# Cross-attention with a quantised feed-forward: the front of each batch one step earlier, and programs of their own for the last three steps

## The chip, the cores and the metric

One core of one Trainium2 chip runs the whole kernel in one launch. The metric is the device time of that launch in microseconds. The engines are PE (TensorE, matmuls and turns by matmul), DVE (VectorE), ACT (ScalarE), POOL (GpSimd) and SP (SyncE, which here only issues DMAs). Each has its own program and runs it in order; they meet by semaphores.

## The reference

Eight batches of 256 tokens by 512 features go through an attention layer and a feed-forward layer, each with a residual:

```python
x = x + attention(layernorm(x), ctx)      # 32 heads of 16, 8 groups: 4 query heads share one K, V head
x = x + ffn(layernorm(x))

# attention: q = X @ Wq.T + bq; k, v from ctx; softmax(q k / 4 with two masks) v; @ Wo.T + bo
# ffn:
h = silu(bitlinear(x, w1, b1))            # 512 -> 2048
h = gelu(h)
h = layer_norm(h, ln_g, ln_b)
return bitlinear(h, w2, b2)               # 2048 -> 512

def bitlinear(x, w, b):                   # x: rms_norm, then 8 bit by row; w: -1, 0, 1 times mean |w|
    return act_quant(rms_norm(x)) @ weight_quant(w).T + b
```

The weights' scales (mean of |w1| and of |w2|) and their rounding to -1, 0 and 1 are computed in the kernel too.

## The kernel before

The work on a batch is cut in four parts, and the program runs eleven steps, n from -1 to 9. In step n four batches are handled at once, one in each part: `a` = n+1 in the front, `c` = n in the scores, `f` = n-1 in the hidden layer, `t` = n-2 in the last layer. `over_batches` (L209) calls each engine's `body(c, a, f, t)`; a part whose batch does not exist is left out. So step -1 has only a front, steps 2 to 6 are full (step 1 lacks the last layer), step 7 has no front, step 8 no scores, and step 9 only the last layer.

- Front, PE: `turn_x` (L538) turns the normalised x by 8 matmuls with the identity, `project_q` (L558) makes Q in 32 matmul records (fp32), `project_kv` (L569) K and V. ACT moves them out of PSUM (`turned_x` L835, `queries` L839, `keys_and_values` L848); DVE makes the rests for a split of Q and K in three bf16 parts (`query_rests` L1057, `key_rests` L1073). SP writes the parts to DRAM (`query_parts` L260, `key_parts` L266) and reads them back with 96 rows of split parts per head (`rows_back` L272, half of the heads at a time). `scores_1` (L585) multiplies Q and K, 16 tiles per batch in a ring of three PSUM tiles, and DVE takes each row's maximum (`maximum` L1086).
- Scores: DVE splits the maxima (`maximum_parts` L1092), PE turns them (`turn_max` L608), DVE copies them (`max_rows` L1108), and SP sends them through DRAM into rows of Q (`maxima` L287). Then `scores_2` (L616) on PE, the exps on ACT (`exps` L860, 16 per batch) and `values` (L632) on PE into PSUM tile PV. ACT copies four pieces out (`values_out` L867); SP collects denominators and numerators (L295, L301); DVE takes reciprocals (L1113), SP spreads them through DRAM (L308), POOL multiplies (`divide` L429).
- Hidden layer: `project_out` (L647), `residual_1`, layer norm and quantising on DVE (L1117 to L1187), `turn_xq` (L660), `layer_1` (L685) in 8 groups, silu, gelu and the sum of squared deviations on ACT (L886 to L912).
- Last layer: DVE scales (`spread_3`, `gain`, `shift`, `maximum_2`, `factor_2`, `scale_2`, L1196 to L1265), ACT takes squares (L913), PE turns (`turn_hq` L704), DVE brings them back (`turn_2` L1266), PE multiplies (`layer_2` L727), DVE adds (`residual_2` L1275), SP stores.

The order on each engine is written by hand. On PE (L742), a step is: `turn_x`, `project_out` first half, `turn_max`, `project_q`, `project_out` second half, `project_kv`, then scores and values by head group with `turn_xq` at group 5 and `turn_hq` at 7, then a loop of 16 in which `scores_1` is mixed with `layer_1` (first 8) and `layer_2` (last 8). x turned, Q, K and V, the hidden layer and the last layer share the PSUM tile FF. On ACT (L922) the order is `turned_x`, `squares(t, 0)`, `queries`, `squares(t, 1)`, `keys_and_values`, exps, silu, gelu.

Step -1 has its own parts: all first loads are issued by SP (L222 to L240), PE does `turn_x(0)`, `mask_flag`, `project_q(0)`, `project_kv(0)`, `scores_1(0, ...)`. Step 0 sums |w1| (ACT, `weight_abs_sum` L879) and rounds w1 (DVE, `quantise_weight` L1021), and folds the V bias into the output bias (`output_bias` L529, 8 matmul records). w2 is loaded behind the reciprocals of batch 0 on SP (`second_weights` L346), into the buffer that held w1. Steps 8 and 9 run `last_body_of` (L783) on PE and `last_body` (L1286) on DVE.

## Time and profile before

| | us |
|---|---|
| median of 3 runs | 649.64 |
| lowest, highest | 649.58, 653.53 |
| the profiled execution | 653.53 |
| its span, first to last instruction | 651.7 |

Over the span PE is busy 538.0 us (83%), DVE 483.8 (74%), ACT 349.2 (54%) and POOL 135.6 (21%). The granted clock of PE is 0.900 on the mean, where 1 is 2.4 GHz; it takes the levels 1.2 and 2.4 GHz. In the profile, rows are groups of instructions: the line of the kernel, the engine, the operation, the tile written and the tiles read. "Idle before" is the time in which the engine stood still ahead of them, with the instruction or DMA that ended it. The chain is followed back from the last instruction, at each step to what released it. Times are from the start of the span.

### The profile page before, as it was taken

What the parts mean: (1) busy time and instruction counts of PE and PEld (TensorE: products, weight loads), DVE (VectorE), ACT (ScalarE), POOL (GpSimd) and SP (SyncE); (2) the same over time, 40 slices, a digit from 0 to 9 for tenths busy, and PEclk for the clock granted to TensorE, in tenths of its full rate; (3) what the DMA queues carried; (4) which work ended last, traced back from release to release, by engine and by line L of the source; (5) the groups of instructions that cost most, each with busy time, mean ns of one, the idle gap of its engine ahead of it and who ended that gap; (6) DMA issues with size and microseconds to landing.
All of it is one profiled execution on the core that took longest, in us unless ns stands there. A gap on an engine that the chain in (4) does not pass through costs nothing.

```text
span 651.7 us, 8896 instructions
## 1 busy us (share of the span) xinstructions
PE 538.0 (83%) x3374; PEld 295.6 (45%) x3374; DVE 483.8 (74%) x717; ACT 349.2 (54%) x424; POOL 135.6 (21%) x102
## 2 busy tenths in 40 slices
PE   2828879778899899999999999999999969954716
PEld 1613733444256445645564557355636514421412
DVE  4339246917879988997899789978988897075494
ACT  1123137053766777386748574956585577818220
POOL 5020004100142052105110511052030312130020
PEclk9865779589998999999999999999999969968668
DMA  8384334785341453265136413641344111200000
GB/s 311 120 227 178 123 89 88 232 312 186 79 112 39 160 131 87 70 201 127 50 120 191 106 61 135 169 98 50 114 125 99 46 40 31 72 0 0 1 33 32
DMA packets 32935, 72.44 MB, mean 111 GB/s; under 512 B 7238, under 2 KB 14406, under 8 KB 29796
## 3 DMA queue, kind: packets, MB, share of 16 engines
q1 hardware_dynamic: 32892, 71.86, 37.1%
q8 instruction: 28, 0.46, 0.3%
q14 instruction: 15, 0.12, 0.1%
HBM read 46.77 MB, written 20.62 MB: 103 GB/s over the span
## 4 chain that ended last, share of the span: by engine, by line
PE 60%; DVE 15%; ACT 7%; issue 7%; DMA 6%; SPq 3%; POOL 1%; DVEq 0%; ACTq 0%
PE FF L737 9%; PE FF L699 9%; PE FF L564 9%; PE PV L656 6%; ACT PT L864 5%; PE PV L642 5%; DVE negm L1089 4%; PE S L604 4%; PE S L628 4%; PE FF L576 3%; PE FF L723 2%; PE FF L580 2%; PE FF L701 2%; PE PV L604 2%; DMA work<-in_w 2%
## 5 line engine op out<-in xcount | busy, mean ns | idle before, releaser
L864 ACT ACTIVATE PT<-S 128x1024 f32<-128x1024 f32 x128 | 123.5, 1034 | 25.5 <-PE S L628 25.5
L1089 DVE TENSOR_REDUCE negm<-S 128x4 f32<-128x1024 f32 x88 | 105.4, 1213 | 25.8 <-PE S L604 24.4
L628 PE MATMUL S<-Q,K 100*128 100x512 bf16 x256 | 74.6, 396 | 14.3 <-ACT PT L864 9.8
L604 PE MATMUL S<-K,Q 97*128 97x256 bf16 x352 | 60.5, 303 | 16.4 <-DMA K<-neg_d 12.5
L642 PE MATMUL PV<-PT,vaug 128*32 128x256 f32 x1024 | 70.3, 393 | 2.7 <-DVE x L1123 2.1
L737 PE MATMUL FF<-w2t,work 128*128 128x512 bf16 x256 | 67.1, 400 | 3.3 <-DVE work L1271 3.3
L699 PE MATMUL FF<-w1t,xqT 128*128 128x512 bf16 x256 | 67.5, 386 | 1.0 <-DVE inv6T L1194 0.6
L564 PE MATMUL FF<-xnT,wq_sb 128*128 128x256 f32 x256 | 63.8, 413 | 4.4 <-ACT xnT L837 4.4
L895 ACT ACTIVATE work<-FF,s 128x512 f32<-128x512 f32 x56 | 38.5, 687 | 39.3 <-PE FF L701 39.3
L656 PE MATMUL PV<-wo_sb,num 128*128 128x512 f32 x128 | 58.8, 604 | 0.0
L564 PEld LDWEIGHTS FF<-xnT,wq_sb 128*128 128x128 f32 x256 | 52.9, 210 | 12.7 <-ACT xnT L837 4.5
L604 PEld LDWEIGHTS S<-K,Q 97*128 97x128 bf16 x352 | 35.0, 105 | 42.5 <-issue 13.4
L1089 DVE TENSOR_REDUCE negm<-PV 128x4 f32<-128x1024 f32 x40 | 48.8, 1219 | 6.6 <-PE PV L604 6.2
L919 ACT ACTIVATE work<-work 128x2048 bf16<-128x2048 f32 x14 | 26.7, 1908 | 41.1 <-DVE work L1208 41.1
L628 PEld LDWEIGHTS S<-Q,K 100*128 100x128 bf16 x256 | 18.3, 99 | 62.3 <-ACT PT L864 44.3
L642 PEld LDWEIGHTS PV<-PT,vaug 128*32 128x32 f32 x1024 | 26.9, 110 | 40.9 <-issue 27.1
L416 POOL TENSOR_TENSOR s<-s,const 128x2 f32<-128x2 f32 (+1 forms) x17 | 11.4, 686 | 156.7 <-DVE s L1135 127.7
L416 POOL TENSOR_TENSOR st<-st,const 128x1 f32<-128x1 f32 (+1 forms) x24 | 25.0, 1040 | 73.1 <-DVE st L1198 64.4
L416 POOL TENSOR_TENSOR num<-num,rec 128x1024 f32<-128x1024 f32 x8 | 18.9, 2362 | 101.2 <-DMA rec<-rec_d 101.2
L737 PEld LDWEIGHTS FF<-w2t,work 128*128 128x128 bf16 x256 | 25.8, 102 | 28.6 <-issue 6.3
L416 POOL TENSOR_TENSOR rs<-rs,const 128x2 f32<-128x2 f32 x8 | 5.6, 698 | 153.6 <-DVE rs L1049 153.6
L1208 DVE SCALAR_TENSOR_TENSOR work<-work,st,b_bc 128x2048 f32<-128x2048 f32 x14 | 32.9, 2351 | 4.1 <-POOL st L416 3.0
(154 smaller groups left out, 843.8 us busy)
## 6 DMA issues: line engine op xcount, KB each, us to landing
Q<-q_d SPq DMA_DIRECT2D x16, 768.0 KB
work<-in_w SPq DMA_DIRECT2D x8, 1024.0 KB, 9.7
q_d<-part SPq DMA_DIRECT2D x8, 768.0 KB, 3.6
x_sb<-in_x SPq DMA_DIRECT2D x8, 512.0 KB, 3.8
ctx_sb<-in_ctxT SPq DMA_DIRECT2D x8, 512.0 KB, 4.0
q_d<-part SPq DMA_DIRECT2D x8, 512.0 KB, 3.2
xb_sb<-in_x SPq DMA_DIRECT2D x8, 512.0 KB, 4.4
rec<-rec_d SPq DMA_DIRECT2D x32, 128.0 KB, 2.7
```

Source lines behind the costliest of these rows:

```text
L416: pool.tensor_tensor(out_, in0, in1, op).then_inc(S[signal], 1)
L564: last = pe.matmul(FFr[:, r, :], wq_sb[:, k, r * P:(r + 1) * P], xnT[:, k, :], start=(k == 0), stop=(k == KD - 1))
L604: last = pe.matmul(to[:, r, :], Q[0:ROWS_1, g, r, t * P:(t + 1) * P], K[0:ROWS_1, g, :], start=not masked, stop=True)
L628: last = pe.matmul(where, K[0:ROWS_2, g, kt * P:(kt + 1) * P], Q[0:ROWS_2, g, 2 * pair:2 * pair + 2, :], start=not masked, stop=True)
L642: last = pe.matmul(PV[32 * r:32 * r + 32, g % 4, :], vaug[:, c % 2, kt, g, :], PT[:, n % PT_SLOTS, r, :], start=(kt == 0), stop=(kt == TT ...
L656: last = pe.matmul(PVw[:, 512 * t:512 * (t + 1)], num[:, g, t * P:(t + 1) * P], wo_sb[:, g, :], start=(g == 0), stop=(g == R - 1))
L699: pe.matmul(FF[:, n % 2, :], xqT[:, k, t * P:(t + 1) * P], w1t[:, k, cols], start=(k == 0), stop=False)
L737: last = pe.matmul(FF[:, tok, :], hqT[:, k, tok * P:(tok + 1) * P], w2t[:, k, :], start=(k == 0), stop=(k == KI - 1))
L864: act.activation(PT[:, n % PT_SLOTS, :, :], ST[n % 2][:], ACT.Exp, scale=0.25).then_inc(S["pt_made"], 1)
L895: act.activation(h_of(f)[:, t, c * 512:(c + 1) * 512], FF[:, n % 2, :], ACT.Silu, scale=s2[:, 7, t:t + 1]).then_inc(S["silu_made"], 1)
L1089: dve.tensor_reduce(negm[:, t, R * g:R * g + R], RING_1[n % 3][:], AX.X, ALU.max, negate=True).then_inc(S["max_made"], 1)
L1208: dve.scalar_tensor_tensor(out=h_of(t)[:, tok, :], in0=h_of(t)[:, tok, :], scalar=st[:, 4, tok:tok + 1], in1=b_bc[:], op0=ALU.mult, op1=AL ...
```

## The change

1. **The first loads.** SP loads x, ctx, wkv and wq in this order (before: x, wq, ctx, wkv); biases, masks and b1 are issued by ACT.
2. **The front one step ahead.** Turning x and projecting Q are done for `w = a + 1`, with K and V still for `a`. Step -1 therefore turns x and projects Q for batches 0, 1 and 2, and K and V for 0 and 1; step 0 has no front; from step 1 on each step does x and Q of n+2; step 6 has neither. K and V of batch 0 come first. Batch 1's x and Q use PSUM tile S0, K and V of batches 0 and 1 use S1. Turning x of batch 2 and its Q are put between the tiles of `scores_1(0, ...)`. Rows of batch 0 come back in three loads, the first with heads 0 and 1.
3. **Step 0.** The sum of |w1| goes to a column of PV; `output_bias` moves between tiles 3 to 9 of `scores_1(1, ...)`, and its addition on DVE to the 13th maximum; POOL divides before it adds the bias to x.
4. **Step 7** has a program of its own. DVE copies the maxima ahead of the first gain and does `residual_1` earlier; `project_out(7)` comes between groups 4 and 5 of `layer_1(6)`. The second half of batch 7's values is not copied out by ACT: DVE turns each 32x32 block from PV, divides by the denominator there and turns back, and SP and ACT send it by DMA into `num`.
5. **Steps 8 and 9**: the sums of `layer_2` go to S0 and the turned hidden values to S1, not to FF; half of `layer_2(5)` stands between groups of `layer_1(7)`; x1 of batch 7 lives in `xb_sb`; the statistics of batch 7 are taken token half by token half.

```diff
             sp.dma_start(x_sb[:], x[0]).then_inc(S["x_in"], 16)
-            sp.dma_start(wq_sb[:], wq).then_inc(S["w_q"], 16)
             sp.dma_start(ctx_sb[:], ctxT[0]).then_inc(S["ctx_in"], 16)
             sp.dma_start(wkv_sb[:], wkv).then_inc(S["w_kv"], 16)
...
+            sp.dma_start(wq_sb[:], wq).then_inc(S["w_q"], 16)
...
+                if at_start(a):
+                    load_context(1)
+                    load_x(1)
+                    key_parts(0)
+                    load_x(2)
+                    query_parts(0)
+                    negatives()
+                    rows_back_first()
+                    weight_chunk(w1, 2)
+                    weight_chunk(w1, 3)
+                    query_parts(1)
+                    key_parts(1)
+                    weights_and_biases()
+                    return
...
             def body_of(c, a, f, t, masked):
-                if a is not None:
-                    turn_x(a)
+                w = next_front(a) if c != 0 else None
+                if w is not None:
+                    turn_x(w)
                 if f is not None:
                     project_out(f, 0, c)
                 if c is not None:
                     turn_max(c)
-                if a is not None:
-                    project_q(a)
+                if w is not None:
+                    project_q(w)
                 if f is not None:
                     project_out(f, 1, c)
-                if a is not None:
+                if a is not None and a > 1:
                     project_kv(a)
...
+                if c is not None:
+                    project_out(f, 0, c)
+                    turn_max(c)
+                    project_out(f, 1, c)
+                    for g in range(G + 1):
+                        if g < G:
+                            scores_2(c, 2 * g, masked)
+                            scores_2(c, 2 * g + 1, masked)
+                        if g > 0:
+                            values(c, 2 * g - 2)
+                            values(c, 2 * g - 1)
+                        if g == 5:
+                            turn_xq(f, None)
+                    for n in range(4):
+                        turn_hq(t, n, f)
+                    for n in range(4):
+                        layer_1(f, n, t)
+                    project_out(c, 0, None)
+                    project_out(c, 1, None)
+                    for n in range(4, 8):
+                        layer_1(f, n, t)
+                    layer_2_last(t, 0)
+                elif f is not None:
+                    turn_xq_last(f)
+                    layer_1(f, 0, None)
+                    layer_1(f, 1, None)
+                    layer_2_last(t - 1, 1)
+                    for n in range(2, 8):
                         layer_1(f, n, None)
                     for n in range(4):
-                        turn_hq(t, n, f)
...
+                        turn_hq_last(t, n)
+                    for tok in range(TT):
+                        layer_2_last(t, tok)
...
                 for n in range(16):
                     scores_1(0, n, masked)
+                    if n == 2:
+                        turn_x(2)
+                    if n in (5, 8, 11, 14):
+                        project_q(2, [(n - 5) // 3])
...
+            project_kv(0)
             turn_x(0)
+            project_q(0)
             mask_flag()
-            project_q(0)
-            project_kv(0)
+            turn_x(1)
+            project_q(1)
+            project_kv(1)
...
+                if c is not None:
+                    squares(t, 0)
+                    act.activation(table_call[:, 1:2], table_call[:, 0:1], ACT.Exp)
+                    for n in range(16):
+                        exps(c, n)
+                        if n == 3:
+                            squares(t, 1)
+                        if n in (5, 9):
+                            values_out(c, (n - 5) // 4)
+                    numerators_last(0)
+                    numerators_last(1)
...
+            def normalise_last(c, j):
+
+                dve.wait_ge(S["pv_made"], 16 * c + 4 * j + 12)
...
+                dve.transpose(turned[:, cols], PVw[:, cols]).then_inc(S["v_turned"], 1)
+                dve.wait_ge(S["v_turned"], j + 1)
+                dve.reciprocal(last_rec[:, j, :], blocks[:, :, HD]).then_inc(S["v_rec"], 1)
+                dve.wait_ge(S["v_rec"], j + 1)
+                dve.tensor_tensor(blocks[:, :, 0:HD], blocks[:, :, 0:HD],
+                                  last_rec[:, j, :].unsqueeze(2).broadcast_to([P, 16, HD]), ALU.mult
+                                  ).then_inc(S["v_scaled"], 1)
+                dve.wait_ge(S["v_scaled"], j + 1)
+                dve.transpose(turned_back[:, cols], turned[:, cols]).then_inc(S["v_back"], 1)
...
+            def last_scores(c, f, t):
+
+                maximum_parts(c)
+                spread_3(t)
+                max_rows(c)
+                gain(t, 0)
+                residual_1(f, 0)
+                shift(t, 0)
+                residual_1(f, 1)
+                norm_2(f)
+                gain(t, 1)
+                shift(t, 1)
+                centre_2(f)
+                scale_1(f)
+                quantise_1(f)
+                bias_scale(f)
+                maximum_2(t, 0)
+                power_2(t)
+                turn_1(f)
+                maximum_2(t, 1)
+                factor_2(t)
+                scale_2(t)
+                reciprocal_last(c)
+                normalise_last(c, 0)
+                normalise_last(c, 1)
+                for n in range(4):
+                    turn_2(t, n)
```

## Rows read from the trace of the kernel before

**Rows 1.** Stages of the span: length, busy us (instructions) by engine, clock, DMA share, GB/s
```profile
61.00:137.00 76.00, 60.83 (x321) 33.84 (x318) 43.83 (x58) 27.30 (x35) 9.51 (x5) 0.75 0.49 149
137.00:207.00 70.00, 59.92 (x370) 34.09 (x371) 49.44 (x73) 38.79 (x49) 15.60 (x10) 0.93 0.45 134
389.20:452.00 62.80, 60.26 (x421) 34.27 (x421) 55.88 (x86) 41.82 (x51) 16.25 (x11) 1.00 0.42 116
514.20:566.90 52.70, 45.73 (x295) 18.79 (x294) 34.12 (x55) 35.53 (x42) 11.49 (x8) 0.90 0.17 44
566.90:620.00 53.10, 31.55 (x130) 14.57 (x128) 30.79 (x49) 22.88 (x26) 6.94 (x6) 0.74 0.03 10
```
**Rows 2.** Chain that ended last, first 137 us: start, length, what
```profile
26.59 3.64 PE FF L576 x8
30.24 1.80 PE FF L580 x16
...
38.88 5.47 DMA K<-neg_d
44.49 1.03 PE S L604 x4
45.54 18.20 DVE negm L1089 x16
65.70 9.70 PE FF L564 x32
...
85.74 6.56 PE FF L535 x8
...
125.03 11.23 DMA work<-in_w
```
**Rows 3.** Two stretches, PE alone: length, busy us (instructions), granted clock, DMA share, GB/s
```profile
44.00:48.00 4.00, 3.51 (x17) 0.50 0.99 259
72.00:77.00 5.00, 3.38 (x16) 1.00 0.00 0
```
**Rows 4.** The same chain, full steps and drain
```profile
393.81 6.96 PE FF L564 x32
...
451.98 1.07 PE FF L554 x8
...
566.86 6.88 PE PV L656 x16
...
610.26 8.83 PE FF L737 x32
...
619.96 0.09 DVE st L1198
```
**Rows 5.** Timeline, steps 0 and 7: start, busy, engine, line, what [idle before <-releaser]
```profile
66.05 0.31 SPq L290 DMA_DIRECT2D m_d<-mT  x1
...
520.62 0.33 SPq L290 DMA_DIRECT2D m_d<-mT  x1
...
525.41 1.89 PE L628 MATMUL S<-Q,K 100*128 100x512 bf16 x4 [3.50 <-DMA Q<-m_d]
...
531.94 1.93 PE L642 MATMUL PV<-PT,vaug 128*32 128x256 f32 x16 [2.14 <-DVE x L1123]
```
**Rows 6.** Timeline of ACT in step 6
```profile
465.06 1.91 ACT L919 ACTIVATE work<-work 128x2048 bf16<-128x2048 f32 x1 [0.64 <-DVE work L1208]
...
471.16 3.78 ACT L864 ACTIVATE PT<-S 128x1024 f32<-128x1024 f32 x4
```
**Rows 7.** Groups of instructions by line: busy us, mean ns of one, idle before
```profile
L1208 DVE SCALAR_TENSOR_TENSOR work<-work,st,b_bc 128x2048 f32<-128x2048 f32 x14 | 32.9, 2351 | 4.1 <-POOL st L416 3.0 <-DVE work L1202 0.5
L416 POOL TENSOR_TENSOR num<-num,rec 128x1024 f32<-128x1024 f32 x8 | 18.9, 2362 | 101.2 <-DMA rec<-rec_d 101.2
L1263 DVE TENSOR_SCALAR work<-work,s 128x2048 f32<-128x2048 f32 x14 | 17.3, 1280 | 0.0
L1123 DVE TENSOR_TENSOR x<-PV,xb_sb 128x512 f32<-128x512 f32 x16 | 10.9, 682 | 5.4 <-DMA out<-x 2.8 <-PE PV L656 2.6
```

589 lines of the change are left out of this document (397 added, 192 removed).

## Prediction

> **What bounds the kernel now.** I read the busy table by stage first. A step n handles four batches at once: the front of n+1, the scores of n, the hidden layer of n-1, the last layer of n-2. The reader is to see three regimes. In a full step PE is busy 60.3 of 62.8 us at full clock: PE is the bound. In the fill (two stages of 76 and 70 us) and the drain (52.7 and 53.1) it is busy for a part only, at a granted clock of 0.74 to 0.93 [rows 1]. So a change that keeps the work the same can pay only in fill and drain.
>
> Then the chain that ended last, through the fill [rows 2]: Q of batch 0 stands ahead of its K and V (from 26.59), then a DMA round to 44.35, then 16 maxima on DVE in 18.20 us (1.14 each, to 63.74). Q of batch 1 (9.70), its K and V, and the eight output-bias matmuls (6.56, to 92.30) then stand ahead of the scores of batch 0, with DVE and ACT mostly idle. The last w2 chunk lands at 136.26; ACT, which sums it, holds up the next front. The clock rows add that the maxima run at granted clock 0.50 (1.2 GHz) although PE is busy 3.51 of 4 us there, and that a dense projection brings back 1.00 (2.4 GHz) by 72 [rows 3].
>
> **Fill, first stage.** K and V of batch 0 need only ctx and wkv and now run beside LN1; they took 3.64 and 1.80 [rows 2]. Turning x waits for them, so Q of batch 0 starts where it did and q_d is written as before: no gain there. load_x(2) stands ahead of query_parts(0) on SP and waits for turn_x(1), about 26; the Q rests come later still, so it costs nothing. New on PE is the work of batch 1: the turn of x, Q (9.70 cold, 6.96 warm [rows 2, 4]), K and V (5.4 cold, by the same ratio 3.9 warm), so PE comes free between 38 and 42.5. Rows come back in three loads, the first with two heads; the last load of the first half took 5.47 [rows 2], and half the bytes land some 2 sooner, at 38 to 40. The first maximum waits for query_rests(1) and key_rests(1) too, so it starts between 39.5 and 44.6 (before 45.54). I take 41.
>
> Between the 16 maxima now stand the turn of x and Q of batch 2. DVE needs 18.2. PE needs 16 tiles of half a cold 1.03, 1.07 for the turn and 6.96 for Q: 16.3 if warm; if cold 16.5 + 2.1 + 9.7 = 28.3 [rows 2, 4]. PE is dense from about 8 on, so I take warm, with 1.8 of bubbles: the maxima end at 61 (cold bound 73).
>
> **Fill, batch 0.** Step 0 now has no front. From the last maximum (63.74) to the issue of the maxima rows (66.05) are 2.3; the DMA round to the first scores takes 4.8, from 520.62 to 525.41 [rows 5]. Scores start at 61 + 7.1 = 68.1, before at 92.30. PE idles some 5 us there: 1.5 for a cold start. From the scores' start to the last w2 chunk nothing is shortened: the same exps, the same chain on SP (denominators, numerators, rows, reciprocals, and only then w2). That took 136.26 - 92.30 = 44.0. query_rests(2) and quantising w1 hide under the exps on ACT; without that cover quantising would stop the whole step. The output bias now lies between the scores of batch 1, whose wait for rows hides its 6.56 on PE; its addition on DVE costs up to 1. Sum 68.1 + 1.5 + 44.0 + 1 = 114.6 against 136.26: 21.7, **take 21** (bounds 10, with the cold first stage, and 25). Steps 1 to 5 have the same work in the same order, with batch a+1 in place of a in the front, and only shift.
>
> The Trainium skill has a rule against one part: in "DMA: Bandwidth & Descriptors", section "Issuing engines are not separate DMA queues", loads started from two engines share the same 16 DMA engines and save only issue time. By it, biases and masks on ACT bring no byte sooner. I gave that move no term, so the sum would be the same; no row here shows it.
>
> **Step 6.** Turn and projection of x fall out (1.07 + 6.96 [rows 4]), since Q of batch 7 came in step 5. PE was the bound, so 8 us seem due. But ACT is late next: squares(4, 1) stands ahead of the exps, waits for DVE's second shift and starts at 465.06 anyhow. With the table load and the K/V copies behind it the exps start at some 469.4 instead of 471.16 [rows 6]. **Gain 2** (bounds 1 and 5).
>
> **Drain.** Times from the start T of step 7 (before 514.2; the end is T + 137.5). DVE copies the maxima rows ahead of the first gain, so the DMA round ends at T + 9.4 instead of T + 11.2, but squares(5, 0) waits for a shift that ends at T + 9.8, and with squares and table load the exps start at T + 13.4. The stall of the values for residual_1 (2.14, till T + 17.7) goes [rows 5]. Sixteen exps of 0.95 [rows 6], one squares and two copies put the last values at T + 33. On DVE turn_1 waits for PE until T + 27; behind it come maximum_2 (a pass over 2048 columns, at most 2.35), small factors, scale_2 (2 x 1.28 [rows 7]) and a reciprocal, to T + 34.6. Then for each half two block turns, a reciprocal and a product. No row has a turn; nearest are DVE reading 128x512 from PSUM, 0.68, as the low end, and the pass over 2048 columns, 2.35, as the high end [rows 7]. By size I take the first, 1.9 per half with the small ones, 3.8 (bounds 3 and 11). By the Trainium skill, "VectorE: DVE Perf Modes", section "The three transpose paths", VectorE turns only 32x32 blocks, 128 bf16 columns in 311 ns: an estimate of 1.2 for 512 columns and of 6 for the two halves.
>
> They stand ahead of turn_2(5, ...) and so of layer_1(6), which starts at T + 41; PE was idle 5 us, so 2.5 more for cold (as 9.70 against 6.96). Four groups, then project_out(7), 6.88 [rows 4], from T + 47 to T + 54. Its inputs are there: numerators about T + 42.3, POOL's division (2.36 [rows 7]) about T + 41.7. Before, it started at 566.86, T + 52.7, behind all of layer_1(6) and layer_2(5) [rows 4]. The rest of layer_1(6) and half of layer_2(5) now cover LN2 and quantising of batch 7, and turn_xq(7) comes at T + 62.5 (before T + 66.2). From there: silu done T + 77.5, squares(6, 1), table, gelu(7, 0) at T + 81. DVE meanwhile does gain, shift, maximum, scale and turns of batch 6, to T + 89, and goes straight on with batch 7. Before, it waited for layer_2(6) (8.83) and both residuals and began batch 7 at 619.96, T + 105.8 [rows 4]; these 17 us are the gain proper. The last step took 31.7 from there; now it holds the residuals of batch 6 too, 33.5. End T + 122.5: **gain 15** (bounds 5 and 22).
>
> **Sum.** 21 + 2 + 15 = 38. The profiled execution took 653.5 (span 651.7) and would take 615.5; the median run is 649.6, 3.9 less, so 649.6 - 38 = **612**.
>
> **Rivals.** *Cold first stage:* PE stays at half clock through the first stage, as before [rows 3]. The maxima end at 73, the fill gains 10: 623. For it: 0.50 at 88% busy before. Against: PE is dense from 8 to 40 now. *Drain gives little:* the turns at their dearest, 7 more ahead of layer_1(6), and the numerators behind them; 5 of 15 remain: 622. *More:* the drain keeps its clock up and step 6 gains 5: 604. *Slower than before:* the half clock lasts through the first stage, batch 0 and batch 1's maxima. From 27 on some 57 us of warm PE work (Q, K, V 11; tiles, turn and Q 16; scores and values 16; tiles and bias 12) take 114, plus 8 of DMA waits: that ends near 150, where 130 was before: 20 lost in place of 21 won. Step 1 at half clock as well adds 40 or so: 650 + 20 + 40 - 17 = 693. It decides once the half clock costs over 38, that is with 76 us of dense work at 0.50 that ran at 1.00 before. Against: 1.00 was back by 72 [rows 3].
>
> **Chances.** Forecast (606 to 618) 0.57; cold first stage 0.14; drain gives little 0.14; both (633) 0.03; more 0.07; slower 0.03; a gain that cancels to within 1% 0.02. About 1% is what a measurement of this kernel can tell from no change. The range 602 to 626 leaves out 0.08 above and a little below. Faster 0.95, same 0.02, slower 0.03.
>
> **What would show it.** K and V matmuls from 7 to 12; first maximum near 41, last near 61, granted clock near 1.0 between; scores of batch 0 from 68; last w2 chunk near 114; full steps still 62.8; step 6 near 60; in the drain exps at T + 13, turn_xq(7) at T + 62, spread of batch 7 at T + 89, end at T + 122. A full step off 62.8 by over 1, or a first maximum after 45, would make the prediction wrong.

## The result and the profile after

| | before | after |
|---|---|---|
| median of 4 runs, us | 651.59 | 620.75 |
| lowest, highest | 649.58, 654.38 | 618.71, 622.59 |
| the profiled execution, its span | 653.53, 651.7 | 622.59, 620.8 |

The ratio is 0.9523, with an interval of 0.9464 to 0.9582: faster, by 31 us where 38 were forecast. 620.75 lies inside the range of 602 to 626 and 8.75 above the 612. Of these 8.75, 2.0 are the kernel before, which ran at 651.59 here and at 649.64 in the runs that the forecast started from; 7 are gain that did not come.

The stages of the changed kernel (length, busy us and instructions by PE, PEld, DVE, ACT, POOL, then PE's granted clock, DMA share, GB/s):

```profile
0.00:62.00 62.00, 44.28 (x234) 37.27 (x234) 40.82 (x73) 18.70 (x30) 14.90 (x20) 0.94 0.76 256
62.00:117.40 55.40, 40.12 (x254) 17.15 (x254) 39.71 (x52) 23.23 (x26) 9.54 (x5) 0.82 0.65 195
117.40:182.50 65.10, 54.18 (x341) 29.63 (x342) 42.63 (x62) 35.92 (x45) 12.86 (x9) 0.88 0.45 137
182.50:247.65 65.15, 62.61 (x421) 35.54 (x420) 57.30 (x88) 44.37 (x55) 16.24 (x11) 0.96 0.38 104
...
310.43:373.22 62.79, 60.24 (x420) 34.24 (x421) 55.89 (x86) 41.80 (x51) 16.22 (x11) 1.00 0.42 116
...
436.00:498.50 62.50, 54.74 (x382) 27.70 (x381) 53.27 (x74) 39.42 (x46) 11.73 (x8) 0.92 0.30 75
498.50:560.00 61.50, 49.52 (x299) 20.71 (x298) 42.80 (x85) 37.68 (x41) 12.17 (x8) 0.89 0.12 33
```

The full step is what it was (62.79 against 62.80 in [rows 1], same busy times). The first stage ran at 0.94, not at the half clock. Step 6 (the row from 436.00) has 5.5 us less of PE work than a full step and is hardly shorter: PE now waits there. From its first instruction on PE to that of step 7 it took 62.6 (435.44 to 498.02), and 62.4 before (451.98 to 514.40).

Matching starts of steps in the two traces (the turn of x that opens step 3 at 263.64 and 247.65, the starts of steps 6 and 7, the ends) splits the 30.9 us of span: **fill 16.0 (forecast 21), steps 3 to 6 0.4 (forecast 2), drain 14.5 (forecast 15)**. None of the 0.4 lies in step 6 itself.

The chain through the fill:

```profile
39.72 2.12 issue
41.83 1.86 PE S L735 x8
...
63.47 0.33 PE S L742 x2
63.82 0.30 DVE mT L1359
64.13 3.16 DMA m_d<-mT
67.31 3.35 DMA Q<-m_d
70.70 1.05 PE S L759 x2
...
105.80 12.48 DMA work<-in_w
118.33 1.79 issue
120.12 0.19 ACT PT L1087
120.31 0.91 ACT xnT L1039
121.26 3.78 PE FF L678 x8
```

The rows of Q and K have landed at 39.72, the first score tile starts 2.12 later, and nothing that the profile shows lies between. The maxima's DMA round takes 6.5 us (3.16 + 3.35), in step 7 of before 4.8 [rows 5]. Last comes the w2 chunk, at 118.28.

Timeline of PE where it comes back from a wait, in steps 6 and 7, and in step 7 where DVE hands it the turned h:

```profile
454.85 1.95 PE L759 MATMUL S<-Q,K 100*128 100x512 bf16 x4 [7.51 <-ACT PT L1069]
456.72 1.94 PE L775 MATMUL PV<-PT,vaug 128*32 128x256 f32 x16
...
512.01 1.95 PE L759 MATMUL S<-Q,K 100*128 100x512 bf16 x4 [3.63 <-ACT PT L1069]
...
537.04 1.86 PE L867 MATMUL FF<-identb,work 128*128 128x128 bf16 x16 [5.40 <-DVE work L1555]
538.93 1.86 PE L853 MATMUL FF<-w1t,xqT 128*128 128x512 bf16 x4
...
545.01 7.03 PE L792 MATMUL PV<-wo_sb,num 128*128 128x512 f32 x16
```

Each time the first rows cost 1.9 for what costs 1.04 to 1.07 at the full clock: PE idled and came back at 1.2 GHz (granted clock 0.50 from 454.85 to 458.60 and from 537 to 541).

### The profile page after: what moved, and what is told of

Read it like the earlier page. It is cut to its first block, busy times and chain, and to the rows that moved or that the text cites. A ratio compares the mean times of both kernels' runs of the same rounds, so it can differ in the third digit from the quotient of the medians.

```text
span 620.8 us, 8914 instructions
## 1 busy us (share of the span) xinstructions
PE 524.9 (85%) x3374; PEld 289.5 (47%) x3374; DVE 489.0 (79%) x728; ACT 350.8 (57%) x424; POOL 135.0 (22%) x101
## 4 chain that ended last, share of the span: by engine, by line
PE 58%; DVE 12%; DMA 10%; ACT 9%; issue 7%; SPq 2%; POOL 1%; ACTq 1%; DVEq 0%
PE FF L853 9%; PE FF L678 7%; PE PV L792 7%; PE FF L901 6%; ACT PT L1069 5%; PE PV L775 5%; PE S L759 5%; PE S L735 5%; DVE negm L1337 4%; PE S L888 3%; PE FF L855 2%; PE PV L735 2%; DMA work<-in_w 2%; PE FF L867 2%; DMA num<-o_raw 2%
## 5 line engine op out<-in xcount | busy, mean ns | idle before, releaser
L1069 ACT ACTIVATE PT<-S 128x1024 f32<-128x1024 f32 x128 | 123.6, 1033 | 28.1 <-PE S L759 28.0
L1337 DVE TENSOR_REDUCE negm<-S 128x4 f32<-128x1024 f32 x88 | 105.6, 1215 | 24.7 <-PE S L735 23.2
L759 PE MATMUL S<-Q,K 100*128 100x512 bf16 x256 | 78.0, 413 | 27.7 <-ACT PT L1069 18.3
L775 PE MATMUL PV<-PT,vaug 128*32 128x256 f32 x1024 | 71.8, 400 | 0.4 <-ACT PT L1069 0.4
L678 PE MATMUL FF<-xnT,wq_sb 128*128 128x256 f32 x224 | 52.8, 394 | 8.6 <-ACT xnT L1039 8.6
L735 PE MATMUL S<-K,Q 97*128 97x256 bf16 x352 | 54.5, 282 | 6.6 <-issue 3.5
L678 PEld LDWEIGHTS FF<-xnT,wq_sb 128*128 128x128 f32 x224 | 43.4, 198 | 15.0 <-ACT xnT L1039 5.8
L775 PEld LDWEIGHTS PV<-PT,vaug 128*32 128x32 f32 x1024 | 27.4, 112 | 40.9 <-issue 27.1
L487 POOL TENSOR_TENSOR s<-s,const 128x2 f32<-128x2 f32 (+1 forms) x17 | 13.5, 803 | 146.7 <-DVE s L1384 114.1
L487 POOL TENSOR_TENSOR num<-num,rec 128x1024 f32<-128x1024 f32 (+1 forms) x8 | 18.8, 2354 | 113.0 <-DMA rec<-rec_d 113.0
L901 PE MATMUL FF<-w2t,work 128*128 128x512 bf16 x160 | 41.1, 378 | 0.0
L792 PEld LDWEIGHTS PV<-wo_sb,num 128*128 128x128 f32 x128 | 24.8, 199 | 26.3 <-issue 25.6
L853 PEld LDWEIGHTS FF<-w1t,xqT 128*128 128x128 bf16 x256 | 24.6, 98 | 24.9 <-issue 3.9
```

The lines of the kernel that those rows point to most:

```text
L487: pool.tensor_tensor(out_, in0, in1, op).then_inc(S[signal], 1)
L678: last = pe.matmul(to[:, r, :], wq_sb[:, k, r * P:(r + 1) * P], xnT[:, k, :], start=(k == 0), stop=(k == KD - 1))
L735: last = pe.matmul(to[:, r, :], Q[0:ROWS_1, g, r, t * P:(t + 1) * P], K[0:ROWS_1, g, :], start=not masked, stop=True)
L759: last = pe.matmul(where, K[0:ROWS_2, g, kt * P:(kt + 1) * P], Q[0:ROWS_2, g, 2 * pair:2 * pair + 2, :], start=not masked, stop=True)
L775: last = pe.matmul(PV[32 * r:32 * r + 32, g % 4, :], vaug[:, c % 2, kt, g, :], PT[:, n % PT_SLOTS, r, :], start=(kt == 0), stop=(kt == TT ...
L792: last = pe.matmul(PVw[:, 512 * t:512 * (t + 1)], num[:, g, t * P:(t + 1) * P], wo_sb[:, g, :], start=(g == 0), stop=(g == R - 1))
```

## Experiments

Every ratio is against the kernel before, run in turns on the same chip; its medians there were 650.1 to 653.5.

### The two halves alone

`a_drain_alone` is the kernel before with the new programs of the last three steps; `b_front_alone` has the new front and the old last steps.

> The front as before (x turned and Q, K, V of a batch in one step, SP issues all first loads), the last three steps as changed. If the two halves of the change are worth what the traces show of each (fill 16.0, steps 3 to 6 0.4, drain 14.5) and don't need each other, this is 651.6 - 14.5 = 637, between 635.5 and 639. If the drain needs the earlier front (step 6 without Q, the PSUM tiles free earlier), less than 10 of the 14.5 stay and it is over 641.

> The front as changed, the last three steps by the old programs. Additive theory: 651.6 - 16.4 = 635, between 633 and 637, the full steps still 62.8 apart. Rival (step 6 without Q, 8 us of PE work less, is a gain that only the old drain would show, or that was lost because of the new one): 627 to 632. The other rival, that the halves overlap in what they save: over 638.

Measured: 637.56 (635.51 to 639.94), ratio 0.9766 (0.9723 to 0.9809); and 635.30 (633.37 to 635.50), ratio 0.9721 (0.9687 to 0.9756). Both lie where the additive theory put them. Against 653.48 these are gains of 15.9 and 18.2. Both together would give 34; the whole change, by its ratio, gives 31, give or take 4. The parts add up within what can be measured, and neither hides the other by more than that.

### What in the drain brings the gain

`g_project_late` moves two lines of PE's program of step 7:

```diff
-                    project_out(c, 0, None)
-                    project_out(c, 1, None)
                     for n in range(4, 8):
                         layer_1(f, n, t)
                     layer_2_last(t, 0)
+                    project_out(c, 0, None)
+                    project_out(c, 1, None)
```

> Undoes the place of the last output projection alone: in step 7 PE does layer_1(6) for n of 4 to 7 and the second layer of batch 5 ahead of project_out(7) and not behind it. As predicted, what ends the drain is the chain project_out(7), residual, turn_xq(7), layer_1(7), gelu, spread: project_out(7) at T+46.9 waits for some 4.3 us of layer_1 and 3.6 us of the second layer, which at T+46.9 have no one waiting: it starts at about T+54, turn_xq(7) at T+69 instead of T+61.5, end 7 us later, 627.5. Rival: project_out(7)'s consumers on DVE are busy until T+58 with the work of batch 5 and 6, so that the place is worth 2 us or less: 621 to 623.

Measured: 640.51 (638.23 to 641.67), ratio 0.9815 (0.9758 to 0.9873), some 19 slower than the changed kernel by the ratios; the theory had said 7, so the direction is right and the size was missed. Its timeline shows why:

```profile
543.88 1.03 PE L853 MATMUL FF<-w1t,xqT 128*128 128x512 bf16 x4
...
551.46 1.89 PE L853 MATMUL FF<-w1t,xqT 128*128 128x512 bf16 x4 [6.33 <-ACT work L1098]
...
559.62 7.03 PE L792 MATMUL PV<-wo_sb,num 128*128 128x512 f32 x16
```

The last two groups of layer_1(6) need PSUM halves that ACT's silu has to read, and ACT does gelu and deviations of the first token half in between. So project_out(7) waits not for 8 us of PE work but for PE's work and ACT's: T = 496.53, and it starts at T + 63.1 against T + 47.0 (T is the first output projection of step 7, 498.02 in the changed kernel). This one placement is worth more than the whole gain of the drain: without it the new last steps are slower than the old ones (ratio 0.9815 against 0.9721 of `b_front_alone`; from T to the end 139.8 against 137.1).

`e_no_block_turns` sends the second half of batch 7's values by the old way. In step 7:

```diff
-                reciprocal_last(c)
-                normalise_last(c, 0)
-                normalise_last(c, 1)
                 for n in range(4):
                     turn_2(t, n)
+                reciprocal(c)
...
-                        if n in (5, 9):
+                        if n in (5, 9, 13):
                             values_out(c, (n - 5) // 4)
-                    numerators_last(0)
-                    numerators_last(1)
+                    values_out(c, 3)
```

with SP's denominators, numerators and reciprocals and POOL's product as in the other steps.

> Undoes the block turns of the last values alone: in step 7 all four pieces of the values of batch 7 go the way of the other batches (copy by ACT, denominators and numerators by SP's DMAs, reciprocal, DMA out and in, product on POOL), and DVE does the four copies of h's turns ahead of the reciprocal. All else of the last three programs stays. In the changed kernel the numerators of the second half land at about T+46 (T the step's first output projection) and project_out(7) starts at T+46.9, behind four tiles of layer_1(6), which would have ended there anyway. Theory: by rows of the old way (copy 0.6, denominators 2.5, reciprocal 0.5, DMA out and in about 5, product 2.6 behind the last exp at T+34) the product is there at T+47 to T+49: project_out(7) 0 to 2 us later, 620.75 to 622.5. Rival 1: the reciprocal's round trip shares the queues with the 4 extra numerator transfers and takes 8 us or more: project_out(7) at T+52, 626. Rival 2: the four tiles of layer_1(6) start 3.8 us earlier with no halves on DVE in front of them, and cold PE is avoided: 618.

Measured: 623.72 (621.13 to 624.85), ratio 0.9549 (0.9508 to 0.9590); the changed kernel has 0.9523, inside the interval. The two ratios tell apart nothing below some 5 us.

```profile
535.31 1.03 PE L853 MATMUL FF<-w1t,xqT 128*128 128x512 bf16 x4
...
542.65 8.96 PE L792 MATMUL PV<-wo_sb,num 128*128 128x512 f32 x16 [6.09 <-POOL num L488]
```

With T = 496.05, project_out(7) starts at T + 46.6. The old way makes PE wait 6.09 for the product behind four groups of layer_1, the block turns make it wait 5.40 ahead of them [the timeline above]; it comes to the same place. From T to the end it is 123.2 against 122.8. The block turns do what they were written for and bring nothing that can be measured.

### Two suspects in the fill

`c_bias_order` issues the V bias on ACT's queue ahead of the masks and not behind them; `d_w2_early` issues all chunks of w2 ahead of the reciprocals of batch 0 and not behind them.

```diff
             act.dma_start(bq_sb[:], bq).then_inc(S["w_bias"], 16)
+            act.dma_start(bv_sb[:], bv).then_inc(S["w_bias"], 16)
             act.dma_start(mq_u8, mask_q).then_inc(S["w_masks"], 16)
...
+                if at_start(c):
+                    second_weights()
                 if c is not None:
                     reciprocals(c)
-                if at_start(c):
-                    second_weights()
```

> The changed kernel with bv issued on ACT right behind bk and bq, ahead of the masks and b1. Theory: K and V of batch 0 lay in PSUM at 14.5 but ACT, which waits for all three biases, copied them only at 16.54, when bv landed, and xnT behind them at 17.16; so Q of batch 0 began at 18.33 and not at 15.2. With bv early Q begins about 15.3 and the first maximum comes 2 to 3 earlier (40 to 41 instead of 42.88), the whole 618 to 619. Rival: the next thing in line (x of batch 1, which landed at 20.5, the Q parts, or the masks, which now land later) keeps the maxima where they are: 620 to 621, first maximum still at 42.9.

> The changed kernel with the four w2 chunks (and b2, g, b) issued on SP right behind the first half of batch 1's rows, not behind the reciprocals of batch 0. Theory: in both kernels ACT waits for the last w2 chunk (136.3 before, 118.3 after) with the turned x of the next batch queued behind its sum; 9 us lie between the last maximum of batch 1 (112.25) and Q of batch 3 (121.26). Loaded early, Q of batch 3 starts at 113 to 114 and the gain of 7 to 8 stays to the end: 612 to 614. Rival: 4 MB in front of denominators, numerators and the second half of the rows delay these by up to 12, the maxima of batch 1 end later, and it comes out at 619 to 624.

Measured: 619.76 (618.11 to 622.57), ratio 0.9484 (0.9452 to 0.9517), and 622.89 (621.38 to 626.96), ratio 0.9552 (0.9502 to 0.9602). By the ratios the first gains 2.5 us, with an uncertainty of 4, so it is not told apart; the second is no gain, as its rival said (619 to 624). In the changed kernel ACT's first K copy stood behind the bias:

```profile
16.54 0.47 ACT L1055 ACTIVATE part<-S,bk_sb 128x256 bf16<-128x256 f32 x1 [9.88 <-DMA bv_sb<-in_bv]
```

In `c_bias_order` that copy starts at 14.15 and Q of batch 0 2.15 earlier, but the first score tile started at 46.24, 4.4 later than in the changed kernel, behind 7.75 us of "issue"; the forecast of a first maximum at 40 to 41 was missed by that. In `d_w2_early` the front no longer waits for w2, but the denominators land behind 4 MB of it, and DVE stands:

```profile
105.25 0.55 DVE L1363 RECIPROCAL denc<-denc 128x64 f32<-128x64 f32 x1 [9.92 <-DMA denc<-x]
```

The maxima of batch 1, behind it in DVE's queue, end at 121.5 and not at 112.25. The order "reciprocals, then w2" protected them: moved w2, the wait changed its owner.

### Orders and the clock in the late steps

`hf_orders` puts the four `turn_2` of step 7 ahead of the block turns, and in step 8 on POOL `mean_3(f, 1)` ahead of `norm_3_last(f, 0)`.

> Two orders are changed, far from each other. In step 7 DVE does the four copies of h's turns (turn_2) ahead of the last reciprocal and the two halves of the block turns, so that PE does not wait 5.40 us at 537.04. In step 8 POOL takes the mean of (7,1) ahead of the power of (7,0). Theory: layer_1(6) starts at T+37 instead of T+40.8, its first silu 3 us earlier; the halves come 2 us later (end T+40 instead of T+38.1), project_out(7) at T+47 as before or 1 us later, so the first order gives 0 to 1. The second takes away 2.7 us (the deviations of (7,1) wait 3.40 for POOL, DVE then 2.72): the spread of (7,1) comes 2.2 us earlier and so does the end. Together 617.5 to 618.5. Rival: the copies ahead delay the halves and so project_out(7) and everything behind it by 2 us, which eats the second: 620.75. Rival for the second: POOL's pow of 2.74 us then lies in front of the spread's next power and the end stays.

Measured: 621.80 (619.44 to 622.33), ratio 0.9517 (0.9474 to 0.9560): no change. The two edits went against each other. The second worked; ACT's second deviations of batch 7, changed kernel and this one:

```profile
589.44 2.00 ACT L1115 ACTIVATE work<-PT,st 128x2048 bf16<-128x2048 f32 x1 [3.40 <-POOL st L487]
```

```profile
588.57 2.00 ACT L1115 ACTIVATE work<-PT,st 128x2048 bf16<-128x2048 f32 x1 [0.30 <-POOL st L487]
```

The wait for POOL fell from 3.40 to 0.30. The first did not: layer_1(6) started at T + 36 (T = 497.91), as expected, but its silu stands on ACT behind the DMAs of the halves, which now came 2.7 us later, and PE waited 6.18 for it; project_out(7) fell back to T + 48.7. What was won on DVE's queue was lost on ACT's.

`w_warm_pe` adds matmuls that nobody reads, where PE idles (`project_kv` of batch 7 does 26 ahead of its own, and stands in step 6 behind the first two score tiles; the 12 and 20 are in the program of step 7):

```diff
+            def spin(where, count):
+                for _ in range(count):
+                    pe.matmul(where, identb[:], mneg_q[:].rearrange("p t n -> p (t n)")[:, 0:where.shape[-1]],
+                              start=True, stop=True)
...
+                if at_start(c):
+                    spin(S1w[:, 0:512], 26)
...
+                    if c == B - 2 and g == 1:
+                        project_kv(a, 26)
...
+                        if g == 0:
+                            spin(FF[:, 1, :], 12)
...
+                    if c == B - 1:
+                        spin(S1w[:, 0:512], 20)
                     turn_hq(t, 2, f)
                     turn_hq(t, 3, f)
```

> Adds matmuls whose results nobody reads, 512 columns each, where PE otherwise idles and comes back at the lower clock: 26 behind the maxima's turns of batch 0 (idle 6.73 before 70.70), 26 ahead of the K and V of batch 7 in step 6, which there are computed behind the first two score tiles (idle 7.51 before 454.85), 12 behind the first two score tiles of step 7 (idle 3.63 before 512.01), 20 ahead of the last two turns of h of step 7 (idle 5.40 before 537.04). Theory 1 (steps 6 and 7 did not gain what was forecast because the exps run into a PE at the lower clock): at the level of 0.21 us a matmul they end before the wait does. The rows of 1.95, 1.94, 1.89 us for four score matmuls behind the wait become 1.03-1.05, ACT's gaps of 1.81 and 1.79 between the exps go, the layer_1 rows of 1.86 and 1.79 become 1.03; step 6 ends 2 us earlier, step 7's layer_1 another 2 to 3 us (T+38), step 0's scores 1 to 2: together 4 to 6, 615 to 617. Theory 2 (the chain there is ACT's and DVE's own, PE's clock is slack): the rows shrink, the ends stay, 620.75 +- 1. Rival 3: the extra matmuls make the clock fall elsewhere or run over into the exps: slower by 1 to 3.

Measured: 628.38 (625.47 to 629.43), ratio 0.9621 (0.9576 to 0.9666): slower by some 6 where 4 to 6 faster was forecast, and its trace has three answers in it. Step 7 onward took 119.5 us against 122.8: the clock there was 1.00 from 505 to 566 and

```profile
545.27 1.02 PE L859 MATMUL FF<-w1t,xqT 128*128 128x512 bf16 x4 [0.28 <-DVE work L1573]
...
549.59 7.03 PE L798 MATMUL PV<-wo_sb,num 128*128 128x512 f32 x16
```

With T = 505.09 project_out(7) starts at T + 44.5. That part is confirmed: a cold PE cost 3.3 us of the drain, or 2.0 to 3.5 if one takes all five kernels with this drain program (121.5 to 123.0 from T to the end in `c_bias_order`, `d_w2_early`, `j_chunks_after_score`, `l_rows_held` and the changed kernel). Step 6 lost 3.0 (65.6 against 62.6), by my own edit: K and V of batch 7 came at 462.07 to ACT, ahead of its exps, which began 23.2 behind the start of the step instead of 18.3. And in the first step PE stood still a second time, for 4.79 us, put down to issue, between the third tile and the turn of x of batch 2. That, with the 7.75 of `c_bias_order`, set the next question.

### The gap that nothing in the profile explains

PE's program has a branch (masks or none) between K/V of batch 1 and the first tile of scores. Before, it was passed while PE waited 12.46 for the rows; now it stands on the path. Part of the idle time behind K/V is still the wait for the rows: in the changed kernel 1.4 of 3.52, K/V ending at 38.31 and the rows landing at 39.72. The first tile started at 41.83 in the changed kernel, then, in the order in which the kernels with this front stand above, at 44.17, 43.85, 43.40, 46.24, 43.51, 44.58 and 42.74, each time behind a 16 KB packet of the instruction queue: in windows of 0.2 us the packet stands 2.6 to 3.1 us ahead of the tile in ten of the eleven kernels and 4.0 in `w_warm_pe`, whose packet also took about twice as long. (The "about 2 us" of the expectations below was read from windows of 2 us.) The queues of the changed kernel in 38:40, then those of the combination below in 46:48 (packets, MB, share of 16 engines):

```profile
q1 hardware_dynamic: 250, 0.52, 98.1%
q8 instruction: 1, 0.02, 3.4%
```

```profile
q1 hardware_dynamic: 93, 0.63, 98.4%
q8 instruction: 1, 0.02, 3.6%
```

`j_chunks_after_score` holds the w1 chunks back until the first tile is computed, `l_rows_held` all but the first rows too (the first and the second edit below):

```diff
                     rows_back_first()
+                    sp.wait_ge(S["s1_ps"], 1)
                     weight_chunk(w1, 2)
...
                                  neg_d[0:1, T * gs.start:T * gs.stop]).then_inc(S[landed], 16)
+                    if landed == "rows_first":
+                        sp.wait_ge(S["s1_ps"], 1)
```

> One wait is added on SP's queue in the first step: chunks 2 and 3 of w1 (1 MB each), and all that stands behind them, are issued only when the first score tile of batch 0 has been computed. Theory 1 (the fill's missing microseconds are a late code fetch): in the changed kernel PE's branch to one of its two programs stands directly between the K/V of batch 1 (ends 38.31) and the first score tile (41.83, idle put down to issue). The trace has one 16 KB packet of the instruction queue q8 in this stretch, between 38 and 40 us, and the tile starts about 2 us behind it; in three other kernels with the same front the packet lies at 40-42, 40-42 and 42-44 us and the tile starts at 44.17, 43.51 and 46.24. The packet queues behind whatever the DMA engines hold, and the two chunks are issued at 39.01 (37.33 in the latest case). Held back, the packet lies at 38-40 in every execution and the first tile starts at 40.5 to 42: gain 1 to 3 us in the median against 620.75 (618 to 620), the slow executions (622) gone. Theory 2 (the fetch queues behind the rows of Q and K, which are issued at 35.57 to 38.69 and stay): nothing changes, the tile starts between 41.8 and 46, time 620.75 +- 1. Theory 3: the idle time is neither, it is PE reading the flag's value: tile at 41.8 in every execution, no gain.

> One wait on SP's queue in the first step, earlier than in the kernel that held only the chunks: of the rows of Q and K of batch 0 only the first two groups (0.48 MB) are read back ahead of the first score tile; the other two shares (0.48 and 0.96 MB), the chunks of w1 and all behind them are issued when that tile has been computed. So far the first tile started at 41.83, 44.17, 46.24, 43.51, 46.16, 42.74, 43.85 and 44.58 in eight kernels with this front, always about 2 us behind a 16 KB packet of the instruction queue q8, and holding the chunks alone changed nothing (46.16). Theory 2 (the code fetch behind PE's branch queues behind the rows of Q and K): with 0.48 MB in front the packet lies at 38 to 40, the tile starts at 40.5 to 42; the rows for tiles 4 and 8 are there in time (0.48 MB take 2 us, a tile 1.1 us). Last maximum 61 to 62, time 618 to 620.5 with few executions over 621. Theory 4 (the gap is the branch's own and does not depend on the DMA engines' load): the tile still starts between 42 and 46; the time is 620.75 to 622, as the held rows cost nothing or 1 us.

Measured: 622.63 (621.52 to 624.27), ratio 0.9533 (0.9489 to 0.9576), tile at 46.16; and 625.93 (624.21 to 627.39), ratio 0.9581 (0.9539 to 0.9622), tile at 41.88. Theory 1 of the first falls: the chunks are not what the packet waits for. Theory 3, PE reading the flag, wanted the tile at 41.8 every time and falls too. With the rows held the packet lies at 38 to 40, as forecast, but it did so in the changed kernel as well. With almost nothing else in the DMA queues (share 0.19 in 38:40, 0.01 in 40:42) the tile still came 3.73 us after K/V and 2.15 after the landing of its rows at 39.73, as in the changed kernel (2.12): that is about the price of the branch itself when the rows land so early. And the held transfers cost more than they gave: PE then waited 1.47 for rows and Q(3) started 60.6 us behind the maxima's turn instead of 57.8. By its ratio the kernel with the rows held is 3.8 us slower than the changed one, with an uncertainty of 5; the one with the chunks held can't be told from it.

### A combination, and the branch turned round

`k_combination`: POOL's order of `hf_orders` alone; the unread matmuls of step 7; 22 of them in step 0; in step 6 K and V back in their place and 40 of 256 columns behind the first two tiles; two chunks of w2 ahead of the reciprocals of batch 0 and two behind. `m_branch_falls_through` is the same with PE's two programs exchanged:

```diff
-            def first_body(general):
-                with pe.If(general):
-                    batches(True)
+            def first_body(plain):
+                with pe.If(plain):
+                    batches(False)
                 with pe.Else():
-                    batches(False)
+                    batches(True)
...
-                dve.tensor_copy(flag_i[:], flag_f[:, 0:1]).then_inc(S["k_flagi"], 1)
+                dve.tensor_copy(flag_i[:], flag_f[:, 1:2]).then_inc(S["k_flagi"], 1)
```

> Four edits at once, each in a place of its own, to be read apart by their times in the trace. (1) POOL takes the mean of (7,1) ahead of the power of (7,0), alone: spread to end 2 to 3 us shorter. (2) Unread matmuls in step 7 as in the kernel with a warm PE (12 and 20), there from T+122.7 to T+119.5. (3) Unread matmuls in step 0 (22 instead of 26, which overran the maxima's DMA round by 0.8) and in step 6, now behind the first two score tiles and with K and V of batch 7 back in their old place (there they delayed the exps to T+22.5; in the changed kernel T+18.25): 40 of 256 columns, 5 us at 0.12, which end before the exps; PE then takes the score tiles at 1.03 instead of 1.9 and step 6 lasts 60.5 to 61.5 instead of 62.6; step 0 1.5 us less. (4) The first two chunks of w2 are loaded ahead of the reciprocals of batch 0, the last two behind: last chunk at turn of the maxima + 49 instead of + 54.8, Q(3) 3 to 5 us earlier. By theory the sum is 2.5 + 3.2 + 3 + 4 = 13: 608 to 611. Rival A: the gaps that close in step 6 and step 0 are slack for the ends of these steps, and the chunks only exchange the wait for another (denominators again): only (1) and (2) stay, 615 to 616. Rival B: the edits in step 0 and 6 cost time: 617 or more.

> The combination, with one thing changed: PE's two programs change places. The branch asks for 'not masked', and the program for plain masks, which this input takes, stands directly behind the branch, the masked one behind it; nothing else moves. Theory (PE's code fetch is the missing part of the fill): in the combination the first tile of scores started at 42.67 (idle 4.50, issue) and PE stood still again from 43.26 to 50.21 (6.96, issue), each time with a 16 KB packet of the instruction queue q8 in the DMA queues near the end of the gap; the maxima of batch 0 turned at 71.28 instead of 63.47 in the changed kernel. All the eleven kernels with this front start the first tile between 41.8 and 46.2, also where the DMA engines had little to do (41.88 with the rows held). With the program standing next in line, its code is on its way before the branch is taken: the tile starts 0 to 2 us behind the landing of the rows (39.8), at 40 to 41.5, no second gap; the maxima turn at 61.5 to 63; the kernel ends at 607 to 611 against 619.16 of the combination. Rival 1: a taken and an untaken branch fetch alike: tile at 42 to 44, the second gap stays or moves by chance: 614 to 619. Rival 2: the program must be fetched in 16 KB packets anyway while the chunks of w1 fill the DMA engines, and the gap moves to the next boundary: tile at 40 to 41.5, one gap of 3 to 7 us later, 613 to 616.

Measured: 619.16 (616.37 to 623.03), ratio 0.9479 (0.9432 to 0.9525), and 613.41 (612.19 to 614.66), ratio 0.9406 (0.9363 to 0.9448). PE around the branch, first the combination, then with the branch turned round:

```profile
42.67 0.58 PE L740 MATMUL S<-K,Q 97*128 97x256 bf16 x2 [4.50 <-issue]
50.21 1.44 PE L740 MATMUL S<-K,Q 97*128 97x256 bf16 x6 [6.96 <-issue]
...
71.28 0.31 PE L747 MATMUL S<-identb,mpart 128*96 128x128 bf16 x2 [3.21 <-DVE mpart L1377]
```

```profile
41.49 1.03 PE L740 MATMUL S<-K,Q 97*128 97x256 bf16 x8 [1.63 <-issue]
...
62.19 0.31 PE L747 MATMUL S<-identb,mpart 128*96 128x128 bf16 x2 [3.21 <-DVE mpart L1377]
```

In the combination PE stood 4.50 and 6.96; in the other 1.63 and nothing more, the tile ran at 1.03 instead of 1.86, no packet of q8 lies between 34 and 52, and the maxima turn 9.1 earlier. PE is no longer last there: DVE starts the first maximum at 42.48 straight behind its own rests, where in the changed kernel it had waited 1.74 for the tile.

The combination missed its forecast of 608 to 611 and lies in the range of rival B (617 or more), though not for rival B's reason. Its trace, apart from the second stop, has nearly the sum that was expected, in other proportions, against the changed kernel: maxima's turn to Q(3) 54.9 instead of 57.8, Q(3) to the first output projection of step 3 124.7 instead of 127.3, step 6 61.9 instead of 62.6, step 7 to the end 117.8 instead of 122.8; 11 in all, of which the late turn of the maxima (71.28, not 63.47) ate 7.8. The 0.7 of step 6 are not a warm PE's. The unread matmuls there ended 3.15 us ahead of the exps, and the score tiles behind them ran cold all the same:

```profile
457.38 1.95 PE L771 MATMUL S<-Q,K 100*128 100x512 bf16 x4 [3.15 <-ACT PT L1093]
```

With the same matmuls step 6 took 63.3 in `m_branch_falls_through`, and without them 61.9 (`c_bias_order`) to 62.9 (`l_rows_held`). What a warm PE would give in step 6 was not shown.

Of the 9.1 that the branch freed, 5.2 reached the end: the scores of batch 0 start 7.8 earlier (70.85 against 78.65), the first output projection then waited 4.03 for POOL's product (3.37 in the combination), and from the maxima's turn to Q(3) it was 58.8 again. The forecast of 607 to 611 was missed by that; 613.41 lies in the range of rival 2, but the later gap that rival 2 expected is not in the trace. The two ratios' intervals overlap by a little (0.9432 to 0.9448), and the executions (616.37 and up, 614.66 and down) don't overlap, though before ran 3.1 lower beside the second; by the ratios the exchange is worth 4.8 us, with an uncertainty of 4, and the traces' 5.2 agrees. This kernel beats the changed one too: ratio 0.9406 against 0.9523. But that is mostly not the branch. Against the changed kernel, which had no second stop, the maxima turn only 1.3 earlier and Q(3) starts 0.3 earlier; of the 8.3 us between the two spans 3.7 lie between Q(3) and step 3 and 5.3 in the drain, and steps 3 to 6 lost 0.9.

Two things speak for code as what PE waits for: the packets lie in the gaps, and the gaps go when the program stands next in line. Two things stay open. A packet alone does not stop PE: nine of the eleven kernels with the old order have one more between 42 and 50 us and run on past it, and only `w_warm_pe` and the combination stopped there. The exchange also moved the plain program to another place in PE's code, and one trace does not tell whether the second stop went by the order or by that place. How long a fetch takes under load was not measured by itself. The Trainium skill has the mechanism, in "Runtime: NRT & Kernel Launch", section "Instruction fetch mechanics": code comes in blocks of 16 KiB, fetched ahead in sequence, and a taken branch to a block that isn't there stops the engine until a DMA has brought it. The traces agree with it, in the packet's size too. That the fetch queues behind the kernel's own transfers is not shown: the packet came 0.3 to 4.8 us behind the end of K/V, and 0.3 was seen with the DMA engines at a share near 1.

## Why the prediction was right, and where it was too high

**Which stages can pay: right.** Full steps stayed at 62.8; 30.5 of the 30.9 us are in fill and drain.

**First stage: nearly right, with two steps wrong.** K and V ran from 8.10 to 14.5 (forecast 7 to 12). My step "Q of batch 0 starts where it did" failed: it started at 18.33 and not at 15.20, and 2.2 of these 3.1 are ACT's wait for a bias (see the last point). The warm clock made that good (Q of batch 1 7.2, PE free at 38.31, forecast 38 to 42.5): the clock stayed up (0.94 over the stage), the rows landed at 39.72 (forecast 38 to 40). The first maximum came at 42.88 (forecast 41) and the last ended at 61.94 (forecast 61). The 1.9 at the start are the branch: my step "the first maximum waits for query_rests(1) and key_rests(1)" is true as far as it goes, the rests ended at 41.15, but DVE then stood 1.74 for the first tile, which PE could start only behind the branch. I had costed the part that moves in front of the branch and not the branch, which before was covered by a wait of 12.46; in other kernels with this front PE stood up to 7.8 there, and with the second gap over 11. The cold first stage (rival, 623) did not happen. That the total lay near its 623 is chance.

**From the last maximum to w2: the term that was short by 4.** The DMA round took 6.5 where I had taken 4.8 from step 7, and with the 0.9 of the last maximum the scores started at 70.70 and not at 68.1. From there to the last w2 chunk it was 47.6, forecast 46.5. Sum: last chunk at 118.28 against 114.6, a gain of 18.0 at that point instead of 21.7. All that the round had more is in its first half, 3.16 against 1.5 in step 7 of before. The load on the DMA engines does not settle it: their share over the round was 0.67 here and 0.07 there, but `g_project_late` has

```profile
65.77 1.49 DMA m_d<-mT
67.28 3.35 DMA Q<-m_d
```

at a share of 0.55, and the combination 3.02 and 3.62 at 0.43. What makes the first half long stays open. In six kernels with this front (the changed one, `b_front_alone`, `d_w2_early`, `e_no_block_turns`, `g_project_late` and `m_branch_falls_through`) the maxima turned between 62.19 and 65.05 and the scores of batch 0 started between 70.61 and 70.92 all the same: within these six an earlier last maximum brought the scores nothing.

**"Steps 1 to 5 only shift": wrong by 2.0.** The gain is 18.0 at Q(3) and 16.0 at step 3. Steps 1 and 2 run at 0.88 and 0.96; PE has gaps there in new places. No experiment took this apart. Part of it is this one execution: the first output projection of step 3 comes at 248.55 here and at 247.4 in `b_front_alone`, `e_no_block_turns` and `g_project_late`, which have the same front and start Q(3) at the same place (121.1 to 121.2), so about half of the 2.0 is not there in them. The combination and `m_branch_falls_through`, with unread matmuls in step 0 and half of w2 early, took 124.7 and 123.6 between Q(3) and step 3, where the others took 125.7 to 128.1, so the clock or w2's place may have a part in it.

**Step 6: mechanism right, size wrong (nothing instead of 2).** ACT was next, as written, and the exps started 18.3 behind the start of the step (before 19.2, forecast 17.4). But the freed 8 us turned into one idle stretch of 7.51 on PE, and behind it the first tiles ran at 1.9 instead of 1.04, and ACT's exps waited 1.81, 0.22 and 0.47 for score tiles. I charged a cold start in step 0 and step 7 and forgot it in step 6. How much of the 2 it took is not shown: in both kernels that tried to keep PE warm at this place with K and V in their old place, the tiles ran cold again, and the step took 61.9 and 63.3.

**Drain: right, 14.5 of 15.** With the forecasts in brackets: exps at T + 12.9 (T + 13.4), layer_1(6) at T + 40.9 (T + 41), project_out(7) at T + 47.0 (T + 47), turn_xq(7) at T + 61.6 (T + 62.5), spread at T + 88.4 (T + 89), end at T + 122.8 (T + 122.5). A block turn of 128x512 took

```profile
L1469 DVE STREAM_TRANSPOSE ctx_sb<-x_sb 128x512 f32<-128x512 f32 x2 | 1.4, 711 | 0.1
L1461 DVE STREAM_TRANSPOSE x_sb<-PV 128x512 f32<-128x512 f32 x2 | 1.3, 660 | 0.0
```

0.66 and 0.71, as the nearest row by size said (0.68), and both halves 4.15 (forecast 3.8). The estimate of 1.2 from the Trainium skill's figure for 128 columns was too high; the trace decides. What I had as "these 17 us are the gain proper" holds, but its cause is the place of project_out(7), not the block turns, which are worth nothing measurable. One cost I missed: POOL's power of (7, 0) ahead of the mean of (7, 1), 3.40 of wait on ACT and 2.72 on DVE; it was made up elsewhere.

**Loads on ACT's queue.** I gave them no term. Whether any bytes came sooner was not tested. But the V bias, 2 KB, issued at 4.67 behind the masks, landed at 16.45 and held ACT's copies of K and V by 2.4 and Q(0) by 2.2, as `c_bias_order` shows; what that would be worth was hidden by the gap behind the branch.

## What to carry to other kernels

When work is moved in front of a point that an engine used to reach early, cost that point too: here a branch that lay under a wait came onto the path once the wait was gone. Put the program that is usually taken directly behind the branch, and expect more from it where PE also stops a second time. Freed time on the bounding engine is worth what the next engine allows; if it turns into idle time, the work behind it can start at half the clock. In a drain look first at which engine's queue stands between two groups of one loop: an operation placed ahead of them (here project_out(7) ahead of the groups that wait for silu) was worth 17 us, and the new way of moving the data nothing that could be measured.

## What the runs showed of the hardware

- At a taken jump PE stood 3.5 to 7.8 us here (2.0 to 3.6 of it behind the landing of the rows in the ten kernels where that can be read), and a second stop of 4.79 or 6.96 came in two of the eleven kernels, with 16 KB instruction packets in the DMA queues beside them; with the usual program next in line it stood 1.63 and did not stop again, in the one trace of it.
- The same small DMA round took 4.8 us at a DMA share of 0.07, 4.9 at 0.55, 6.5 at 0.67 and 6.7 at 0.43: the share alone does not tell its time.
- Unread matmuls in four waits raised PE's mean granted clock from 0.926 to 0.948 (0.952 in the last kernel) and were worth some 3 us in the drain, where they ended 1.1 to 1.3 us ahead of the next real work. In step 6, where they ended 3.15 and 2.90 ahead of it, the tiles behind them ran at 1.95 or soon fell to it.
